# Mamba-style scan kernel: own prologue, own last image and a new instruction order

## The chip, the cores and the metric

The program runs on one core of one Trainium2 chip. The metric is the device time of that core in microseconds (us), the median of several runs. A core has five engines that run in parallel, each through its own list of instructions in strict order: PE (TensorE, matrix products), DVE (VectorE), ACT (ScalarE), POOL (GpSimd) and SP (SyncE, which here only issues DMAs). They wait for each other through semaphores. PE, DVE and ACT reach PSUM, POOL only SBUF.

## The reference, cut to what matters

There are 16 images of 16 x 16 positions (L = 256) with 64 channels. Each goes through a small self-attention with max-pooled keys and values, and a residual. Then it is read in four orders (as it is, columns reversed, rows reversed, both); every order is a sequence of 256 steps through a gated state-space mixer with 128 channels and 16 states per channel. All is fp32.

```
attn = softmax(theta @ maxpool(phi).T);  x = x + sigma * ((attn @ maxpool(g)) @ w_o + b_o)
hs, gate = split(rmsnorm(x) @ W_in.T);   hs = silu(causal_conv4(hs) + conv_b)
dt_r, B, C = split(hs @ W_x.T);          dt = softplus(dt_r @ W_dt.T + b_dt)
state = exp(dt * A) * state + dt * B * hs      # per time step, for 16 states n
y = sum_n(state * C) + hs * Dp
h = x + (y * silu(gate)) @ W_out.T;      out = layernorm(mean of 4 orders of rmsnorm(h))
```

## The kernel before, in words

The four orders of an image lie side by side as one row of T = 1024 elements, the 128 channels are the partitions. Per image and state n (16 states) the kernel needs a decay exp(a_n * dt), an input du * B_n (du = dt * hs), a scan over 1024 elements by DVE (`scan`, L1136 or L1143), a product with C_n, and an addition into `ps_y`, which PE does with identity matmuls (`sum_state`, L582). B_n and C_n come by DMA as 512 KB rows broadcast to 128 partitions (`load_b`, `load_c`).

`KIND = "ACCPACCCCPACPACC"` gives each state its kind:

- C: ACT writes the decay to PSUM (`ps_decay`, L804), POOL makes the input (`scan_input`, L1006), DVE scans in PSUM and DVE multiplies by C_n (`product`, L1150).
- P: the same inputs, but the scan writes to SBUF and POOL multiplies (L1012).
- A: ACT scales eight transposed blocks (`act_input`, L834), PE turns them into PSUM (`turn_input`, L568), the decay goes to SBUF (`sb_decay`, L811), DVE scans, POOL multiplies.

So an image has 16 scans, 9 DVE products, 7 POOL products, 12 POOL inputs and 4 inputs by ACT and PE. States of even and odd n alternate between the two buffers `ps_x[0]` and `ps_x[1]`, so state n can be prepared only when state n-2 has left its buffer.

The order of the work is written out by hand for every engine, in `prologue`, `steps(b, done, coming, later)` and `finish`. While image b is scanned, the image before it (`done`) is gated and normalised (`gated`, `hid_norm`, `out_norm` on DVE, `hid_squares`, `hid_inverse`, `out_squares`, `out_inverse`, `out_copy` on ACT, `hid_proj`, `hid_mean`, `out_mean` and others on PE), the next (`coming`) goes through norm, padding, convolution, gate and softplus, and the one after that (`later`) through its attention. All of these small stages share `ps_w`, whose halves are `w0` and `w1`. ACT changes its function table between Exp/Ln, Silu and Softplus (`silu_table`, `exp_table`, `softplus`).

In the prologue the first image goes through all stages with nothing to overlap. POOL makes its du (`scan_weight`), ACT copies all four parts of the padded input (`pad`), and the attention of the second image uses the first half of `ps_x[1]`. `warm(count)` issues matmuls of a zero tile into `ps_x[0]`, results unused; a matmul of fp32 is two instructions in the trace.

Of the kernel before, what the change touches and what calls it, by code (L numbers as in the profile page):

```python
# [5 lines left out]
ALU = mybir.AluOpType  # L6
# [4 lines left out]
L = SIDE * SIDE  # L11
# [3 lines left out]
N = 16  # L15
# [20 lines left out]
BY_POOL_IN = [n for n in range(N) if KIND[n] in "CP"]  # L36
BY_DVE_OUT = [n for n in range(N) if KIND[n] == "C"]
BY_ACT_IN = [n for n in range(N) if KIND[n] == "A"]
BY_SB_DECAY = [n for n in range(N) if KIND[n] == "A"]
BY_POOL_OUT = [n for n in range(N) if KIND[n] in "AP"]  # L40
NPI, NAI, NDO, NPO = len(BY_POOL_IN), len(BY_ACT_IN), len(BY_DVE_OUT), len(BY_POOL_OUT)
NSD = len(BY_SB_DECAY)
# [37 lines left out]
def build(nc, a, out):  # L80
    ctx = ExitStack()
    with ctx:
# [183 lines left out]
        def attn_bank(j):  # L266


            return ps_x[1][:, 0:HALF] if j.num == 1 else w0

        def product_wait(b, n):

            if n < 0:
                b, n = b + -1, n + N
            if KIND[n] == "C":
                return dve_products, NDO * b.num + BY_DVE_OUT.index(n) + 1
            return pool_products, NPO * b.num + BY_POOL_OUT.index(n) + 1

        def x_free_wait(b, n):

            if n < 0:
                b, n = b + -1, n + N
            if KIND[n] == "C":
                return dve_products, NDO * b.num + BY_DVE_OUT.index(n) + 1
            return scans, N * b.num + n + 1

        def pool_in_index(b, n):
            return NPI * b.num + BY_POOL_IN.index(n)

        def act_in_index(b, n):  # L290
            return NAI * b.num + BY_ACT_IN.index(n)

        def sb_decay_index(b, n):
            return NSD * b.num + BY_SB_DECAY.index(n)

        def scan_count(kind, each, index):

            return N * (index // each) + kind[index % each] + 1 if index >= 0 else 0

        def program(eng, prologue, steps, finish):  # L300

            prologue()
            for i in range(IMAGES):
                steps(Image(i), Image(i - 1) if i > 0 else None, Image(i + 1) if i + 1 < IMAGES else None,
                      Image(i + 2) if i + 2 < IMAGES else None)
            finish(last)
# [3 lines left out]
        def _(sp):  # L313
# [11 lines left out]
            def store_bc(j):  # L325

                all_at_least(sp, (bc_rows_done, j.num + 1), (pool_inputs, NPI * (j.num - 1)),
                             (pool_products, NPO * (j.num - 1)), (dve_products, NDO * (j.num - 1)))
# [4 lines left out]
            def load_b(b, n):  # L333

                i = pool_in_index(b, n)
# [15 lines left out]
            def prologue():  # L351
# [7 lines left out]
                load_c(first, 1)  # L359
                load_b(first, 5)  # L360

            def finish(j):
                store_out(j)

            def steps(b, done, coming, later):
                load_c(b, 2)
                load_b(b, 6)
                load_b(b, 7)
                load_c(b, 3)
                load_c(b, 4)  # L370
                load_b(b, 8)
                load_b(b, 9)
                load_c(b, 5)
                load_c(b, 6)
                if later:
                    load_x(later)
                load_b(b, 11)
                load_c(b, 7)
                load_b(b, 12)
                load_b(b, 14)  # L380
                load_c(b, 8)
                load_c(b, 9)
                load_b(b, 15)
                load_c(b, 10)
                if coming:
                    store_bc(coming)
                load_c(b, 11)
                load_c(b, 12)
                if coming:
                    load_b(coming, 1)  # L390
                    load_b(coming, 2)
                load_c(b, 13)
                load_c(b, 14)
                load_c(b, 15)
                if coming:
                    load_b(coming, 3)
                    load_c(coming, 0)
                    load_b(coming, 5)
                    load_c(coming, 1)
                if done:  # L400
                    store_out(done)

# [5 lines left out]
        def _(pe):  # L408
# [151 lines left out]
            def turn_input(b, n):  # L560

                i = act_in_index(b, n)
                pe.wait_ge(a_scaled, i + 1)
                if b.num == 0 and n % 2 == 1:
                    pe.wait_ge(x2_done, 2)
# [10 lines left out]
            def sum_state(b, n):  # L576

                at_least(pe, *product_wait(b, n))
                if n == 0:
                    at_least(pe, yg_done, 2 * b.num)  # L580
                for half in range(2):
# [5 lines left out]
            def prologue():  # L587
                second = first + 1
                pe.wait_ge(warm_zeroed, 1)
                warm(6)  # L590
                pe.wait_ge(qkv_weights_in, 16)
                qkv(first)
                pe.wait_ge(attn_weights_in, 16)
                scores(first)
                warm(2)
                warm(2)
                attn_turn(first)
                attn_out(first)
# [13 lines left out]
                warm(2)  # L612
                scores(second)
                bt_turn(first)
                warm(1)
                dut_turn(first, 0)
                dut_turn(first, 1)
                attn_turn(second)
                warm(1)
                attn_out(second)  # L620
                turn_input(first, 0)

            def finish(j):
                sum_state(j, 13)
# [5 lines left out]
                hid_mean(j)  # L630
                warm(2)
                warm(2)
                out_mean(j)
                warm(3)
                out_square(j)
# [657 lines left out]
```

## Time and profile before

| | |
|---|---|
| median of 3 runs | 848.98 us (848.57 to 849.10) |
| the profiled execution | 847.56 us |
| its span in the trace | 845.8 us |
| busy: PE, DVE, ACT, POOL | 93%, 93%, 90%, 89% |
| DVE idle until its first scan | 36.63 us |
| after the last product of DVE | 15.2 us |

The profiled execution lies 1.42 us below the median. The trace shows three stretches: a prologue until the first scan at 36.63 us, 15 image periods of about 49.7 us, then the last image (first scan at 782.02 us) and a tail of small steps that follow one another.

In the rows, a line gives the start in us, the duration in us, the engine, the line in the kernel, the operation, out<-in with the shape, and how many instructions were merged. Square brackets hold the idle time of that engine just before, and what ended it.

### The profile page before, as it was taken

What the parts mean: (1) busy time and instruction counts of PE and PEld (TensorE: products, weight loads), DVE (VectorE), ACT (ScalarE), POOL (GpSimd) and SP (SyncE); (2) the same over time, 40 slices, a digit from 0 to 9 for tenths busy, and PEclk for the clock granted to TensorE, in tenths of its full rate; (3) what the DMA queues carried; (4) which work ended last, traced back from release to release, by engine and by line L of the source; (5) the groups of instructions that cost most, each with busy time, mean ns of one, the idle gap of its engine ahead of it and who ended that gap; (6) DMA issues with size and microseconds to landing.
All of it is one profiled execution on the core that took longest, in us unless ns stands there. A gap on an engine that the chain in (4) does not pass through costs nothing.

```text
span 845.8 us, 10516 instructions
## 1 busy us (share of the span) xinstructions
PE 789.4 (93%) x2738; PEld 398.5 (47%) x2738; DVE 787.5 (93%) x537; ACT 759.9 (90%) x1438; POOL 748.6 (89%) x346
## 2 busy tenths in 40 slices
PE   7599999999999999999999999999999999999787
PEld 4335454454544445444454544444454554445343
DVE  2299999999999999999999999999999999999993
ACT  4899999999999999999999999999999999998551
POOL 0499999999989999998999999899999989999980
PEclk7899999999999999999999999999999999999999
DMA  1698999899998898989888898988989899888970
GB/s 46 248 292 295 294 314 300 300 292 307 315 286 308 301 294 284 321 300 310 307 293 293 294 312 305 293 305 309 305 280 312 282 312 312 297 295 293 302 265 6
DMA packets 73706, 240.61 MB, mean 284 GB/s; under 512 B 12848, under 2 KB 16176, under 8 KB 73648
## 3 DMA queue, kind: packets, MB, share of 16 engines
q1 hardware_dynamic: 73648, 239.96, 84.5%
q8 instruction: 22, 0.36, 0.2%
q14 instruction: 36, 0.29, 0.1%
HBM read 236.78 MB, written 3.15 MB: 284 GB/s over the span
## 4 chain that ended last, share of the span: by engine, by line
DMA 23%; ACT 23%; issue 16%; DVE 15%; POOL 13%; PE 8%; SPq 2%; ACTq 0%; DVEq 0%; POOLq 0%
DMA c_all<-bc_dram 13%; ACT scaled L834 10%; DMA b_all<-bc_dram 10%; POOL inp L1006 9%; ACT ps_x L804 6%; DVE state L1136 5%; DVE ps_x L1143 4%; PE ps_y L582 3%; POOL state L1012 3%; DVE state L1150 3%; DVE state L1143 2%; PE ps_w L473 1%; ACT ps_w L721 1%; SPq L343 1%; ACT oln L863 1%
## 5 line engine op out<-in xcount | busy, mean ns | idle before, releaser
L582 PE MATMUL ps_y<-state,packed 128*128 128x512 f32 x1024 | 473.2, 598 | 5.9 <-POOL state L1012 5.8
L1006 POOL TENSOR_TENSOR inp<-du,b_all 128x1024 f32<-128x1024 f32 x192 | 450.4, 2366 | 2.1 <-DMA b_all<-bc_dram 1.9
L1143 DVE TENSOR_TENSOR_SCAN ps_x<-ps_x,inp 128x1024 f32<-128x1024 f32 x144 | 325.6, 2281 | 3.4 <-ACT ps_x L804 3.4
L1012 POOL TENSOR_TENSOR state<-state,c_all 128x1024 f32<-128x1024 f32 x112 | 263.5, 2360 | 36.1 <-DVE state L1136 33.1
L582 PEld LDWEIGHTS ps_y<-state,packed 128*128 128x128 f32 x1024 | 191.4, 191 | 214.4 <-issue 196.9
L804 ACT ACTIVATE ps_x<-step,a_neg 128x1024 f32<-128x1024 f32 x192 | 213.8, 1114 | 43.4 <-DVE state L1150 21.9
L1150 DVE TENSOR_TENSOR state<-ps_x,c_all 128x1024 f32<-128x1024 f32 x144 | 172.2, 1214 | 1.8
L834 ACT ACTIVATE scaled<-dut,bt 128x128 f32<-128x128 f32 x512 | 154.4, 391 | 0.0
L1136 DVE TENSOR_TENSOR_SCAN state<-decay,ps_x 128x1024 f32<-128x1024 f32 x64 | 145.0, 2265 | 9.4 <-PE ps_x L568 9.4
L1143 DVE TENSOR_TENSOR_SCAN state<-ps_x,inp 128x1024 f32<-128x1024 f32 x48 | 109.7, 2285 | 7.5 <-issue 3.5
L568 PE MATMUL ps_x<-packed,scaled 128*128 128x128 f32 x512 | 68.3, 277 | 10.9 <-ACT scaled L834 9.2
L473 PE MATMUL ps_w<-xpad,w_conv 128*128 128x512 f32 x128 | 64.2, 626 | 11.2 <-ACT ocen L858 9.0
L568 PEld LDWEIGHTS ps_x<-packed,scaled 128*128 128x128 f32 x512 | 57.2, 143 | 36.8 <-ACT scaled L834 22.8
L811 ACT ACTIVATE decay<-step,a_neg 128x1024 f32<-128x1024 f32 x64 | 71.2, 1137 | 0.0
L996 POOL TENSOR_TENSOR du<-step,u 128x1024 f32<-128x1024 f32 x16 | 37.8, 2364 | 37.5 <-ACT step L789 37.5
L776 ACT ACT_TABLE_LOAD x46 | 59.0, 1283 | 0.8
L473 PEld LDWEIGHTS ps_w<-xpad,w_conv 128*128 128x128 f32 x128 | 23.9, 197 | 43.1 <-issue 37.1
L773 ACT ACT_TABLE_LOAD x31 | 39.8, 1283 | 0.5
L573 PE MATMUL ps_y<-u,diag_d 128*128 128x512 f32 x64 | 32.7, 593 | 0.0
L486 PE MATMUL ps_w<-u,w_step 128*128 128x512 f32 x64 | 30.3, 595 | 0.5 <-ACT u L769 0.5
L520 PE MATMUL ps_w<-hsq,mean_w 128*128 128x512 f32 x32 | 18.0, 645 | 11.0 <-ACT hsq L842 10.9
L769 ACT ACTIVATE u<-ps_w,packed 128x512 f32<-128x512 f32 x32 | 22.0, 687 | 4.5 <-PE ps_w L473 4.2
(123 smaller groups left out, 622.2 us busy)
## 6 DMA issues: line engine op xcount, KB each, us to landing
c_all<-bc_dram SPq DMA_DIRECT2D x256, 512.0 KB, 5.9
b_all<-bc_dram SPq DMA_DIRECT2D x192, 512.0 KB, 6.4
bc_dram<-bc_rows SPq DMA_DIRECT2D x64, 32.0 KB, 2.2
xa<-in_x_t SPq DMA_DIRECT2D x16, 64.0 KB, 8.1
out<-ofin SPq DMA_DIRECT2D x16, 64.0 KB, 3.8
packed<-in_packed SPq DMA_DIRECT2D x1, 635.0 KB, 4.1
packed<-in_packed SPq DMA_DIRECT2D x1, 129.0 KB, 2.5
w_qkv<-in_w_qkv SPq DMA_DIRECT2D x1, 64.0 KB, 2.0
```

Source lines behind the costliest of these rows:

```text
L473: last = mm(ps_w[:, HALF * half:HALF * (half + 1)], w_conv[:, 2 * half + tap2, :], moved, start=(tap2 == 0), stop=(tap2 == 1))
L568: last = nc.tensor.transpose(ps_x[n % 2][:, 128 * k:128 * (k + 1)], scaled[i % A_RING][:, k, :], ident)
L582: last = mm(ps_y[:, HALF * half:HALF * (half + 1)], ident, state[n % H_RING][:, HALF * half:HALF * (half + 1)], start=(n == 0), stop=(n == ...
L776: act.preload_act_table_set(EXP_LN)
L804: f(ps_x[n % 2][:, :], step[b.buf][:, :], ACT.Exp, scale=a_neg[:, n:n + 1]).then_inc(ps_decay_done, 1)
L811: f(decay[i % D_RING][:, :], step[b.buf][:, :], ACT.Exp, scale=a_neg[:, n:n + 1]).then_inc(sb_decay_done, 1)
L834: last = f(scaled[i % A_RING][:, k, :], dut[b.buf][:, k, :], ACT.Copy, scale=bt[b.buf][:, at, row:row + 1])
L1006: tt(inp[i % IN_RING][:, :], du[b.buf][:, :], b_all[i % B_RING][:, :], ALU.mult).then_inc(pool_inputs, 1)
L1012: tt(state[n % H_RING][:, :], state[n % H_RING][:, :], c_all[n % C_RING][:, :], ALU.mult).then_inc(pool_products, 1)
L1136: v.tensor_tensor_scan(held, decay[i % D_RING][:, :], x, 0.0, ALU.mult, ALU.add).then_inc(scans, 1)
L1143: v.tensor_tensor_scan(held if KIND[n] == "P" else x, x, inp[i % IN_RING][:, :], 0.0, ALU.mult, ALU.add).then_inc(scans, 1)
L1150: v.tensor_tensor(state[n % H_RING][:, :], ps_x[n % 2][:, :], c_all[n % C_RING][:, :], ALU.mult).then_inc(dve_products, 1)
```

## The change

1. **State kinds per image.** `KINDS` gives the first 15 images the old string and the last image `"ACPPAPCCPPAAPACA"`: 6 A, 6 P and 4 C instead of 4 A, 3 P and 9 C. `finish` now holds the whole last image, with an order of its own.
2. **First image.** DVE makes du and sets the stops (`first_weight`), and copies the second of the two padded orders (`first_pad`). DVE's weight preparations come before `rms(first)`. `state_decay` on ACT and `step_weights` on PE come earlier.
3. **Second attention** uses the second half of `ps_y`, which is free until the first `sum_state`; that one now waits for `x2_done` of the second image, and the waits for it in `ps_decay` and `turn_input` are gone.
4. **Zero matmuls** in the prologue: counts 8, 2, 3, 4, 7 where they were 6, 2+2, 1, 2, 1, 1. In the tail 2, 3, 2, 2 where they were 2, 2+2, 3.
5. **Order in `steps`**, for every image, on all five queues.

```diff
+LAST_KIND = "ACPPAPCCPPAAPACA"
+KINDS = [KIND] * (IMAGES - 1) + [LAST_KIND]
-            return ps_x[1][:, 0:HALF] if j.num == 1 else w0
+            return ps_y[:, HALF:T] if j.num == 1 else w0
@@ PE prologue
-                warm(6)
+                warm(8)
                 pe.wait_ge(qkv_weights_in, 16)
                 qkv(first)
+                warm(2)
                 pe.wait_ge(attn_weights_in, 16)
                 scores(first)
-                warm(2)
-                warm(2)
+                warm(3)
+                step_weights()
                 attn_turn(first)
                 attn_out(first)
+                warm(4)
                 pe.wait_ge(zeroed, 9)
                 mean_square(first)
-                step_weights()
-                warm(1)
-                qkv(second)
+                warm(7)
                 pe.wait_ge(conv_weights_ready, 1)
                 conv(first, 0)
                 conv(first, 1)
@@ DVE, new functions
+            def first_pad(j):
+                dve.wait_ge(zeroed, 9)
+                dve.wait_ge(xn_done, j.num + 1)
+                v.tensor_copy(grid(xpad[0:C, 1, 3:3 + L]), ordered(xn[j.buf][0:C, :], 1)).then_inc(padded, 1)
+                v.tensor_copy(grid(xpad[C:, 1, 2:2 + L]), ordered(xn[j.buf][C:, :], 1)).then_inc(padded, 1)
+            def first_weight(j):
+                dve.wait_ge(step_done, j.num + 1)
+                dve.wait_ge(u_done, 2 * (j.num + 1))
+                v.tensor_tensor(du[j.buf][:, :], step[j.buf][:, :], u[j.buf][:, :], ALU.mult).then_inc(du_done, 1)
```

The new order of one image in `steps`, with sN a scan, PN a DVE product, pN a POOL product, iN a POOL input, dN a `ps_decay`, a mark ' for the coming image:

```
DVE before: s0 s1 rms' gated P1 s2 P2 hid_norm s3 s4 s5 s6 P5 P6 s7 s8 P7 P8 s9 s10 s11 P11 pooling s12 s13 row_max s14 out_norm P14 s15 P15
DVE after:  P15(done) s0 s1 s2 gated P1 P2 rms' s3 s4 hid_norm s5 P5 s6 P6 s7 P7 s8 P8 s9 s10 s11 pooling P11 s12 s13 s14 row_max P14 s15 out_norm
ACT before: residual' d1 rms_inverse' d2 sb4 in10 hid_squares pad' hid_inverse d3 silu_table conv_silu0' exp_table d5 out_squares d6 silu_table conv_silu1' gate' exp_table d7 d8 softplus' exp_table bc_copy' d9 sb10 sb13 bt' dut0' d11 d12 theta dut1' in13 in0' d14 out_inverse softmax d15 attn_copy in4' out_copy sb0'
ACT after:  d2 residual' in10 rms_inverse' hid_squares d3 pad' hid_inverse d5 silu_table conv_silu0' exp_table out_squares d6 d7 silu_table conv_silu1' gate' exp_table d8 softplus' exp_table d9 bc_copy' sb10 sb13 d11 bt' dut0' in13 d12 theta dut1' in0' d14 sb0' sb4' out_inverse d15 softmax in4' d1' out_copy attn_copy
POOL before: p3 i8 p4 i9 i11 du' i12 i14 p9 p10 i15 p12 i1' p13 i2' p0' i3' i5' i6' i7'
POOL after:  p3 p4 i8 i9 i11 i12 du' i14 p9 p10 i15 p12 p13 i1' i2' i3' i5' p0' i6' i7'
```

On PE, `attn_out` comes at the head of the next image, `sum_state(13)` and `sum_state(14)` at the end of their own, `sum_state(b, 0)` before `hid_mean(done)`, and `scores(later)` before `turn_input(b, 13)`. On SP the loads are issued in an order that follows the others, some of the coming image's C rows earlier.

The last image, in `finish`:

```
DVE:  P15(done) s0 s1 P1 gated s2 s3 s4 s5 s6 s7 P6 P7 hid_norm s8 s9 s10 s11 out_norm s12 s13 s14 s15 P14
POOL: p2 p3 p4 p5 i8 i9 i12 p8 p9 i14 p10 p11 p12 p13 p15
PE:   ... sum12 sum13 sum14 sum15, then the tail as before
```

## Rows read from the trace of the kernel before

**Rows 1.** The page, busy time of each engine over the whole span.

```profile
PE 789.4 (93%) x2738; PEld 398.5 (47%) x2738; DVE 787.5 (93%) x537; ACT 759.9 (90%) x1438; POOL 748.6 (89%) x346
```

**Rows 2.** Stretches: length, busy PE, PEld, DVE, ACT, POOL, granted clock, DMA share, GB/s.

```profile
11.40:15.80 4.40, 3.41 (x8) 1.75 (x8) 2.27 (x10) 2.61 (x7) 0.00 (x0) 0.51 0.05 15
15.80:21.40 5.60, 5.56 (x7) 2.48 (x8) 1.01 (x5) 2.48 (x4) 0.00 (x0) 0.50 0.00 0
...
633.14:682.95 49.81, 47.93 (x169) 24.27 (x168) 48.82 (x33) 47.55 (x91) 46.70 (x22) 1.00 0.93 301
```

**Rows 3.** Timeline of DVE in a middle image, with its waits.

```profile
613.27 2.29 DVE L1143 TENSOR_TENSOR_SCAN state<-ps_x,inp 128x1024 f32<-128x1024 f32 x1 [0.17 <-issue]
...
633.14 2.29 DVE L1136 TENSOR_TENSOR_SCAN state<-decay,ps_x 128x1024 f32<-128x1024 f32 x1
...
638.11 1.29 DVE L1161 TENSOR_TENSOR yg<-ps_y,gate 128x512 f32<-128x512 f32 x2 [0.18 <-PE ps_y L582]
...
640.44 2.29 DVE L1143 TENSOR_TENSOR_SCAN ps_x<-ps_x,inp 128x1024 f32<-128x1024 f32 x1
642.76 1.23 DVE L1150 TENSOR_TENSOR state<-ps_x,c_all 128x1024 f32<-128x1024 f32 x1
...
644.84 2.29 DVE L1143 TENSOR_TENSOR_SCAN state<-ps_x,inp 128x1024 f32<-128x1024 f32 x1 [0.25 <-POOL inp L1006]
...
656.19 4.48 DVE L1143 TENSOR_TENSOR_SCAN ps_x<-ps_x,inp 128x1024 f32<-128x1024 f32 x2 [0.19 <-ACT ps_x L804]
...
663.09 2.29 DVE L1143 TENSOR_TENSOR_SCAN state<-ps_x,inp 128x1024 f32<-128x1024 f32 x1 [0.17 <-issue]
```

**Rows 4.** Timeline of ACT in the same image.

```profile
640.15 0.60 ACT L842 ACTIVATE hsq<-ps_w 128x512 f32<-128x512 f32 x1
...
654.97 2.25 ACT L804 ACTIVATE ps_x<-step,a_neg 128x1024 f32<-128x1024 f32 x2 [0.37 <-DVE state L1150]
...
659.66 1.28 ACT L776 ACT_TABLE_LOAD   x1
661.07 0.39 ACT L796 ACTIVATE bc_rows<-ps_w 128x256 f32<-128x256 f32 x1
661.88 1.12 ACT L804 ACTIVATE ps_x<-step,a_neg 128x1024 f32<-128x1024 f32 x1 [0.43 <-DVE state L1150]
```

**Rows 5.** Timeline of POOL in the last image: four inputs in a row.

```profile
786.68 9.32 POOL L1006 TENSOR_TENSOR inp<-du,b_all 128x1024 f32<-128x1024 f32 x4
```

**Rows 6.** Timeline of the prologue, PE and ACT.

```profile
1.05 2.93 PE L419 MATMUL ps_x<-warm_zero 128*128 128x128 f32 x12 [1.05 <-DVE warm_zero L1063]
...
3.77 1.05 PE L427 MATMUL ps_w<-xa,w_qkv 128*72 128x256 f32 x2
...
11.42 1.11 PE L458 MATMUL ps_w<-x2sq,mean_w 128*128 128x256 f32 x2 [1.10 <-ACT x L747]
...
15.28 0.41 ACT L762 ACTIVATE xpad<-xn 64x256 f32<-64x256 f32 x1
...
15.84 6.61 PE L473 MATMUL ps_w<-xpad,w_conv 128*128 128x512 f32 x8 [1.00 <-ACT xpad L762]
...
25.81 1.11 ACT L789 ACTIVATE step<-ps_w,packed 128x1024 f32<-128x1024 f32 x1 [0.80 <-PE ps_w L486]
```

**Rows 7.** Timeline of DVE: scan 9 of the first image, scan 0 of the second.

```profile
65.73 2.29 DVE L1143 TENSOR_TENSOR_SCAN state<-ps_x,inp 128x1024 f32<-128x1024 f32 x1 [0.16 <-issue]
...
85.37 2.28 DVE L1136 TENSOR_TENSOR_SCAN state<-decay,ps_x 128x1024 f32<-128x1024 f32 x1
```

**Rows 8.** Timeline of the last image, DVE and PE.

```profile
782.02 2.28 DVE L1136 TENSOR_TENSOR_SCAN state<-decay,ps_x 128x1024 f32<-128x1024 f32 x1
...
827.09 5.55 PE L582 MATMUL ps_y<-state,packed 128*128 128x512 f32 x12
...
829.38 1.22 DVE L1150 TENSOR_TENSOR state<-ps_x,c_all 128x1024 f32<-128x1024 f32 x1
...
832.68 1.29 DVE L1161 TENSOR_TENSOR yg<-ps_y,gate 128x512 f32<-128x512 f32 x2 [2.08 <-PE ps_y L582]
```

More of the change, by code:

```diff
@@ L35, with numbered, scans_until, before @@
 KIND = "ACCPACCCCPACPACC"
[L36 to L42, printed above, removed]
+LAST_KIND = "ACPPAPCCPPAAPACA"
+KINDS = [KIND] * (IMAGES - 1) + [LAST_KIND]
+def numbered(kinds):
+    return {key: i for i, key in enumerate((b, n) for b in range(IMAGES) for n in range(N) if KINDS[b][n] in kinds)}
+def scans_until(table, index):
+    return next(N * b + n + 1 for (b, n), i in table.items() if i == index) if index >= 0 else 0
+def before(table, num):
+    return sum(1 for b, n in table if b < num)
+POOL_IN, ACT_IN = numbered("CP"), numbered("A")
+DVE_OUT, POOL_OUT = numbered("C"), numbered("AP")
 EXP_LN, SILU, SOFTPLUS = "natural_log_exp_and_others", "silu_and_others", "softplus"
@@ L611, in prologue @@
                 step_proj(first, 0)
-                warm(2)
+                bt_turn(first)
+                qkv(second)
+                dut_turn(first, 0)
                 scores(second)
-                bt_turn(first)
-                warm(1)
-                dut_turn(first, 0)
                 dut_turn(first, 1)
+                turn_input(first, 0)
                 attn_turn(second)
-                warm(1)
-                attn_out(second)
-                turn_input(first, 0)
             def finish(j):
+                done = j + -1
+                sum_state(done, 15)
+                hid_residual(done)
+                hid_proj(done)
+                hid_mean(done)
+                turn_input(j, 4)
+                sum_state(j, 0)
+                sum_state(j, 1)
+                sum_state(j, 2)
+                sum_state(j, 3)
+                sum_state(j, 4)
+                sum_state(j, 5)
+                out_mean(done)
+                sum_state(j, 6)
+                out_square(done)
+                turn_input(j, 10)
+                skip(j, 0)
+                sum_state(j, 7)
+                turn_input(j, 11)
+                sum_state(j, 8)
+                sum_state(j, 9)
+                out_final(done)
+                turn_input(j, 13)
+                skip(j, 1)
+                sum_state(j, 10)
+                turn_input(j, 15)
+                sum_state(j, 11)
+                sum_state(j, 12)
                 sum_state(j, 13)
@@ L668, in steps @@
                 sum_state(b, 6)
+                turn_input(b, 10)
                 if coming:
                     bt_turn(coming)
-                turn_input(b, 10)
+                skip(b, 0)
                 if coming:
                     dut_turn(coming, 0)
-                skip(b, 0)
-                if later:
-                    qkv(later)
                 sum_state(b, 7)
@@ L679, in steps @@
                     dut_turn(coming, 1)
+                if later:
+                    qkv(later)
                 sum_state(b, 8)
-                sum_state(b, 9)
-                turn_input(b, 13)
                 if later:
                     scores(later)
+                turn_input(b, 13)
+                sum_state(b, 9)
                 if done:
@@ L697, in steps @@
                 if later:
-                    attn_out(later)
+                    attn_turn(later)
+                if done:
+                    out_final(done)
+                sum_state(b, 13)
+                sum_state(b, 14)
             program(pe, prologue, steps, finish)
@@ L933, in steps @@
                 ps_decay(b, 6)
+                ps_decay(b, 7)
                 if coming:
@@ L1195, in steps @@
             def steps(b, done, coming, later):
+                if done:
+                    product(done, 15)
                 scan(b, 0)
                 scan(b, 1)
-                if coming:
-                    rms(coming)
+                scan(b, 2)
                 if done:
```

309 lines of the change are left out of this document (193 added, 116 removed).

## The prediction, made before the changed kernel had run

> **What bounds the kernel now.** I read the page's busy times first [rows 1]: four engines lie between 89% and 93%, so none can be picked by its share alone. The stretches come next. In a middle image of 49.81 us DVE is busy 48.8 us, PE 47.9, ACT 47.6 and POOL 46.7 [rows 2]. DVE has about 1 us left, but it is not all there is: a timeline of DVE shows four short waits in the image, of 0.17 to 0.25 us, for PE, POOL and ACT [rows 3]. Each costs a little more than it shows, since the overlap with the next instruction is lost too (scan 3 starts 0.33 us later than its work asks), about 1.2 us together. DVE is the bound, with ACT right behind it: the reader should see that ACT runs 21.7 us from `hid_squares` to the decay of state 9 with waits of only 0.37 and 0.43 us [rows 4]. The last place is the prologue: no scan until 36.63 us, and in it a convolution of 6.61 us at half the granted clock [rows 2, 6].
>
> So the change has four accounts: prologue, first image, 14 middle images, last image. The sum goes by the profiled execution (span 845.8 us, time 847.56 us); the median of the runs is 1.42 us above it, and I add that at the end.
>
> **Prologue.** All steps from the first matmul to the end of softplus (26.92 us, [rows 6]) follow one another, so each counts in full.
> - 8 instead of 6 zero matmuls stand ahead of `qkv(first)`. Twelve instructions ran from 1.05 to the start of `qkv` at 3.77; they are 0.21 us apart, so four more cost 0.85 us. If the clock rises meanwhile, `qkv`'s two instructions (1.05 us) give up to 0.4 back. I take +0.7.
> - The zero matmuls and `step_weights` behind `qkv`, `scores` and `attn_out` fall in waits of PE for ACT and DVE; nothing late. The preparations of weights that DVE now does before `rms` take some 3 us and stand in DVE's idle time before it; the two earlier small steps of ACT likewise.
> - `mean_square` took 1.11 us at the half clock (0.51 in this stretch, [rows 2]); at full clock half of it: -0.5.
> - ACT makes two of four pads, DVE the others beside it. No row has a copy of 64x256 by DVE from SBUF; ACT's takes 0.41 [rows 6]. Between nearly nothing and the same as ACT it stays hidden: -0.9.
> - `conv(first)`: eight instructions at 0.85 us. The clock was at 0.50 from 11.5 us on, after a stretch in which PE had little to do, and it rose only at 21.5 us, after 5.7 us without a gap [rows 2]. With 4 and 7 zero matmuls around `mean_square` (8 and 14 instructions, 0.9 and 1.5 us at full clock, both shorter than the waits that they fill) PE has work in about two thirds of that time. In the tail of the last image, where zero matmuls stand in the same way, it kept the full clock. Then the convolution takes 8 x 0.43 = 3.4 us: -3.0.
> Sum -3.7 us. The other end: the clock falls all the same. Then seven zero matmuls take 14 x 0.21 = 3.0 us and delay the convolution by some 0.5 us, but PE works without a gap from 12.1 us on, the clock comes back in the middle of the convolution, and the net is -1.8; at worst +0.4.
>
> A rule of the Trainium skill bears on it, in "TensorE: Matmul & The Clock Gate", Part 1: the throttled clock is the default, activity of the array releases it, and the moment varies from run to run. By that rule zero operands do as well as real ones, and the prologue gives the 3.7 us; the same section makes the amount uncertain from run to run. The rows of the convolution agree with the first half.
>
> **First image.** From the end of softplus ACT has its work nearly without a gap until the decay of state 9: scan 9 started 38.8 us behind softplus, scan 0 of the second image another 19.64 us later [rows 7, 6]. DVE's du is 1.2 us faster than POOL's 2.3 (no row has it from two SBUF operands; the product of 1.22 us from PSUM is nearest, [rows 8]), and POOL gets one input more before its first product, but ACT is what is late next, and its list holds the same instructions. The copy of B and C rows now comes behind the decay of state 9 (0.4 us), and two product waits go later in the image (below, 0.24 us). I take -0.8, between 0 and -2.
>
> **Middle images.** DVE's own list is the same in content; removed waits could give 1.1 us per image. But the order adds waits of its own. I work the loop out from scan 0:
> - Scan 0 to `gated`: three scans at 2.19 us apart (the pair in [rows 3], less overlap) instead of two scans and `rms`: 6.57 us; before, it was 638.11 - 633.14 = 4.97.
> - `gated` to `hid_squares` on ACT, by PE's projection: 640.15 - 638.11 = 2.04 us.
> - From `hid_squares` to the decay of state 9 ACT has the very same instructions before and after (decays 3, 5, 6, 7, 8, pads, `hid_inverse`, both convolution Silus, gate, softplus, five table loads), only `bc_copy` has gone behind. Before: to the end of the last table load 659.66 + 1.28 - 640.15 = 20.79 us, less the wait of 0.37 = 20.42. The decay itself 1.10 and 0.12 to the start of the scan: 21.64 us.
> So scan 9 starts 6.57 + 2.04 + 21.64 = 30.25 us behind scan 0. By DVE's own work it could start at about 29.1 us: DVE now waits about 1.1 us for ACT, in two parts, before scan 6 (some 0.5, for decay 6, which stands behind the first Silu block) and before scan 9 (some 0.5). Before it was 663.09 - 633.14 = 29.95.
> - Scan 9 to the next scan 0: 633.14 - 613.27 = 19.87 us before. Products 11 and 15 no longer stand right behind their own scans; a product right behind costs 2.32 us from scan to product [rows 3] against 2.19: 19.87 - 0.24 = 19.63.
> The period is 30.25 + 19.63 = 49.88 us against 29.95 + 19.87 = 49.82. Over 14 images +0.8 us. PE's, POOL's and SP's parts have room in this timing: `hid_mean` is ready about 0.5 us before ACT asks, `turn_input(13)` 0.4 us before scan 13, loads of C are issued 7 us or more ahead. Range -0.3 to +0.3 us an image, that is 4 us each way.
>
> **Last image.** Five products go from DVE to POOL, two inputs from POOL to ACT and PE. DVE loses 5 x 1.13 us. POOL gains: behind scan 13 of image 14 it has p13, five operations of transition (four inputs, p0), and 16 more until p13 of the last: 22 at 2.32 us [rows 5] = 51.0 us without a gap. Scan 13 ends 5.7 us before P15 of image 14, so p13 of the last image ends 45.4 us behind the start of that P15. Then PE adds three states, 12 instructions in 5.2 us [rows 8]: 50.6. Before, the same stretch ran from 780.9 (1.14 before scan 0) to 832.4, 0.3 before `gated`: 51.5 [rows 8]. Gain -0.9 us: POOL takes DVE's place as the bound. If POOL were earlier, DVE would set it, with its stalls for decays and for `turn_input(11)` (1.6 us by the same walk): scan 15 ends at 44.2, its product by POOL 2.4, a sum 1.7: 48.3, so -3.2. The other end is 0. The tail behind keeps its steps; the zero matmuls there stand in waits: 0.
>
> **Sum.** -3.7 - 0.8 + 0.8 - 0.9 = -4.6 us. 847.56 - 4.6 = 843.0 for a profiled execution, 844.4 against the median.
>
> **Rivals.**
> 1. *The clock is not kept in the prologue.* For it: between `mean_square`'s zero matmuls and the pads PE still has about 1 us idle, and it fell there before. The prologue gives 1.8 or nothing: 846.3 to 848.5.
> 2. *ACT does not bind the middle images*, DVE runs without waits at about 48.8 us: another 14 x 1.0 us, 830. Against it speaks that ACT's 47.6 us plus its waits for scan 0 (0.6) and for the projection (1.2) already fill the period.
> 3. *`sum_state(b, 0)` before `hid_mean` makes it slower.* PE now waits for POOL's product 0 before it may run `hid_mean`, and product 0 stands behind four inputs of POOL instead of two. By my walk it ends 8.0 us behind P15, PE asks at 9.7 us, and ACT can bear another 0.6 us. From 10.3 us on, one POOL operation (2.3 us) late, every further tenth goes through `hid_inverse` into the ACT chain above and so into every image. With 0.5 us beyond it: +7 us, 851.4. Against it: POOL has about 2.7 us idle per image with which to catch up.
> 4. *The last image is set by DVE after all*: 842.1.
>
> **Chances.** Forecast 0.53, its own range 840 to 848 (14 images by 0.3 us make nearly all of it); rival 1 0.17; rival 2 0.08; rival 3 0.14; rival 4 0.08. The range reaches from half-way to rival 2 to rival 3: 836.5 to 851.5. A measurement of this kernel can tell 0.2%, 1.7 us, from no change. Faster than 847.3: most of the forecast (0.48), rivals 2 and 4, half of rival 1: 0.72. Slower than 850.7: rival 3, of which a part stays below, and a tail of the forecast: 0.13. Within: 0.15.
>
> **What would show it.** In the prologue: granted clock 1.00 through the convolution and softplus ending near 23.2 us. In a middle image: waits of DVE for `ps_x` of ACT before scans 6 and 9, none of note before 3 and 7; `hid_squares` 8.6 us behind scan 0; a period of 49.6 to 50.2. In the last image: POOL without a gap until its last product, DVE waiting little, first scan to last `gated` near 49.7 us instead of 50.7. The prediction is wrong if the waits before scans 6 and 9 are missing or a third appears, for PE or POOL.

## The result: slower by a quarter of a per cent

| | before | changed |
|---|---|---|
| median of 13 runs each | 849.07 us | 850.71 us |
| ratio of the times | | 1.0024, 95% interval 1.0015 to 1.0033 |
| the profiled execution, its span | 847.56, 845.8 us | 849.61, 847.7 us |
| first scan | 36.63 us | 33.22 us |
| scan 0 of the second image | 85.37 us | 80.92 us |
| from there to scan 0 of the last image, 14 images | 696.65 us | 703.97 us |
| from there to the last `gated` | 50.66 us | 49.69 us |
| tail behind it | 13.1 us | 13.1 us |

The prediction was 844.4 us and faster; the kernel became slower, by 1.6 us in the medians and by 2.0 us in the ratio and in the profiled executions. Each ratio here and below is to runs of the kernel before that were taken together with the experiment (medians of 847.85 to 849.26 us), and it need not be the quotient of the two medians.

The four accounts of the prediction say where. The start gained 4.45 us, the last image 0.97, the tail nothing, and the 14 middle images lost 7.3: together +1.9 us, the difference of the two spans. Of the 7.3 us, 14 times the longer period (50.30 instead of 49.82 us) is 6.7; one of the 14 images took 50.57 us, and what that one waited for was not followed up.

The page of the changed kernel has nearly the same busy times as [rows 1]; DVE has less to do and a longer span around it:

```profile
PE 791.7 (93%) x2772; PEld 403.6 (48%) x2772; DVE 783.2 (92%) x536; ACT 765.7 (90%) x1452; POOL 754.0 (89%) x347
```

The same stretches as in [rows 2]: the first convolution, a middle image, the last image up to its `gated` (columns as there).

```profile
15.38:19.05 3.67, 3.67 (x9) 1.74 (x10) 0.00 (x0) 1.84 (x2) 0.00 (x0) 1.00 0.00 0
...
583.93:634.23 50.30, 48.15 (x169) 24.41 (x168) 48.85 (x34) 47.72 (x92) 46.77 (x22) 1.00 0.85 298
...
784.89:834.58 49.69, 45.66 (x143) 21.15 (x142) 42.17 (x26) 28.17 (x55) 46.48 (x21) 1.00 0.62 217
```

DVE is busy 48.85 us in a middle image, as before; the image is 50.30 us long instead of 49.82. Which waits make up the rest is in DVE's timeline, the counterpart of [rows 3]:

```profile
583.93 2.27 DVE L1236 TENSOR_TENSOR_SCAN state<-decay,ps_x 128x1024 f32<-128x1024 f32 x1
...
590.48 1.26 DVE L1261 TENSOR_TENSOR yg<-ps_y,gate 128x512 f32<-128x512 f32 x2
...
603.55 2.30 DVE L1243 TENSOR_TENSOR_SCAN ps_x<-ps_x,inp 128x1024 f32<-128x1024 f32 x1 [0.73 <-ACT ps_x L853]
...
614.41 2.29 DVE L1243 TENSOR_TENSOR_SCAN state<-ps_x,inp 128x1024 f32<-128x1024 f32 x1 [0.38 <-ACT ps_x L853]
...
630.57 2.30 DVE L1243 TENSOR_TENSOR_SCAN ps_x<-ps_x,inp 128x1024 f32<-128x1024 f32 x1 [0.20 <-ACT ps_x L853]
...
634.23 2.27 DVE L1236 TENSOR_TENSOR_SCAN state<-decay,ps_x 128x1024 f32<-128x1024 f32 x1
```

The waits before scans 6 and 9 (603.55 and 614.41) are the two that were forecast. A third, before scan 15, was not. All three are for a decay by ACT, whose timeline answers to [rows 4]:

```profile
592.49 0.60 ACT L891 ACTIVATE hsq<-ps_w 128x512 f32<-128x512 f32 x1 [0.94 <-PE ps_w L537]
...
613.21 1.12 ACT L853 ACTIVATE ps_x<-step,a_neg 128x1024 f32<-128x1024 f32 x1
...
629.37 1.10 ACT L853 ACTIVATE ps_x<-step,a_neg 128x1024 f32<-128x1024 f32 x1
...
644.67 0.42 ACT L812 ACTIVATE xpad<-xn 64x256 f32<-64x256 f32 x1 [0.26 <-DVE xn L1213]
```

The last of these lines is of the next image; in this one ACT waits the same 0.26 us for `xn`, until 594.36. So the loop is: scan 0 to `gated` 6.55 us, to `hid_squares` 2.01, to scan 9 21.92, to the next scan 0 19.82; sum 50.30. The prediction had 6.57, 2.04, 21.64 and 19.63.

The prologue, PE, DVE and ACT, the counterpart of [rows 6]:

```profile
1.05 3.78 PE L444 MATMUL ps_x<-warm_zero 128*128 128x128 f32 x16 [1.05 <-DVE warm_zero L1149]
...
4.63 1.06 PE L452 MATMUL ps_w<-xa,w_qkv 128*72 128x256 f32 x2
...
12.29 0.67 PE L483 MATMUL ps_w<-x2sq,mean_w 128*128 128x256 f32 x2 [0.21 <-ACT x L798]
12.79 1.72 PE L444 MATMUL ps_x<-warm_zero 128*128 128x128 f32 x14
...
14.45 0.29 DVE L1218 COPY xpad<-xn 64x256 f32<-64x256 f32 x1
...
15.38 3.67 PE L498 MATMUL ps_w<-xpad,w_conv 128*128 128x512 f32 x8 [0.86 <-ACT xpad L813]
...
22.42 1.11 ACT L840 ACTIVATE step<-ps_w,packed 128x1024 f32<-128x1024 f32 x1 [0.80 <-PE ps_w L511]
...
23.57 1.23 DVE L1224 TENSOR_TENSOR du<-step,u 128x1024 f32<-128x1024 f32 x1 [2.61 <-ACT step L840]
```

Every step is there: 0.86 us later at `qkv`, `mean_square` in 0.67 us instead of 1.11, the convolution in 3.67 instead of 6.61, DVE's copies of 0.29 us beside ACT's pads, softplus at its end at 23.53 us instead of 26.92.

DVE's scan 9 of the first image and scan 0 of the second (as [rows 7]):

```profile
61.58 2.29 DVE L1243 TENSOR_TENSOR_SCAN state<-ps_x,inp 128x1024 f32<-128x1024 f32 x1
...
80.92 2.28 DVE L1236 TENSOR_TENSOR_SCAN state<-decay,ps_x 128x1024 f32<-128x1024 f32 x1
```

And the last image (as [rows 8]), with POOL's last products:

```profile
784.89 2.27 DVE L1236 TENSOR_TENSOR_SCAN state<-decay,ps_x 128x1024 f32<-128x1024 f32 x1
...
834.58 1.29 DVE L1261 TENSOR_TENSOR yg<-ps_y,gate 128x512 f32<-128x512 f32 x2 [5.66 <-PE ps_y L606]
...
819.77 11.60 POOL L1086 TENSOR_TENSOR state<-state,c_all 128x1024 f32<-128x1024 f32 x5
```

### The profile page after: what moved, and what is told of

The parts are those of the page before. It is cut to its first block, busy times and chain, and to the rows that moved or that the text cites. A ratio compares the mean times of both kernels' runs of the same rounds, so it can differ in the third digit from the quotient of the medians.

```text
span 847.7 us, 10597 instructions
## 1 busy us (share of the span) xinstructions
PE 791.7 (93%) x2772; PEld 403.6 (48%) x2772; DVE 783.2 (92%) x536; ACT 765.7 (90%) x1452; POOL 754.0 (89%) x347
## 4 chain that ended last, share of the span: by engine, by line
PE 28%; ACT 20%; DMA 16%; DVE 13%; issue 11%; POOL 10%; SPq 2%; DVEq 0%; ACTq 0%; POOLq 0%
PE ps_y L606 13%; DMA b_all<-bc_dram 10%; POOL inp L1080 7%; DMA c_all<-bc_dram 6%; DVE ps_x L1243 6%; ACT ps_x L853 5%; PE ps_w L498 4%; POOL state L1086 3%; DVE state L1250 3%; PE ps_w L537 2%; ACT scaled L883 2%; PE ps_w L511 2%; ACT L827 2%; ACT xpad L813 1%; DVE state L1243 1%
## 5 line engine op out<-in xcount | busy, mean ns | idle before, releaser
L1080 POOL TENSOR_TENSOR inp<-du,b_all 128x1024 f32<-128x1024 f32 x190 | 445.2, 2362 | 44.3 <-DMA b_all<-bc_dram 26.5
L1243 DVE TENSOR_TENSOR_SCAN ps_x<-ps_x,inp 128x1024 f32<-128x1024 f32 x139 | 315.8, 2281 | 13.8 <-ACT ps_x L853 13.8
L1086 POOL TENSOR_TENSOR state<-state,c_all 128x1024 f32<-128x1024 f32 x117 | 273.6, 2358 | 29.5 <-DVE state L1243 28.6
L1250 DVE TENSOR_TENSOR state<-ps_x,c_all 128x1024 f32<-128x1024 f32 x139 | 167.6, 1214 | 2.2
L883 ACT ACTIVATE scaled<-dut,bt 128x128 f32<-128x128 f32 x528 | 161.0, 392 | 0.5
L1236 DVE TENSOR_TENSOR_SCAN state<-decay,ps_x 128x1024 f32<-128x1024 f32 x66 | 149.7, 2268 | 7.7 <-PE ps_x L591 7.7
L1243 DVE TENSOR_TENSOR_SCAN state<-ps_x,inp 128x1024 f32<-128x1024 f32 x51 | 116.2, 2279 | 5.8 <-ACT ps_x L853 5.3
L591 PEld LDWEIGHTS ps_x<-packed,scaled 128*128 128x128 f32 x528 | 61.9, 142 | 32.1 <-issue 27.8
L891 ACT ACTIVATE hsq<-ps_w 128x512 f32<-128x512 f32 x16 | 9.6, 597 | 29.0 <-PE ps_w L537 29.0
L537 PE MATMUL ps_w<-yg,packed 128*64 128x256 f32 x128 | 20.0, 405 | 9.9 <-DVE yg L1261 9.9
```

The costliest lines, as they stand in the source:

```text
L591: last = nc.tensor.transpose(ps_x[n % 2][:, 128 * k:128 * (k + 1)], scaled[i % A_RING][:, k, :], ident)
L883: last = f(scaled[i % A_RING][:, k, :], dut[b.buf][:, k, :], ACT.Copy, scale=bt[b.buf][:, at, row:row + 1])
L1080: tt(inp[i % IN_RING][:, :], du[b.buf][:, :], b_all[i % B_RING][:, :], ALU.mult).then_inc(pool_inputs, 1)
L1086: tt(state[n % H_RING][:, :], state[n % H_RING][:, :], c_all[n % C_RING][:, :], ALU.mult).then_inc(pool_products, 1)
L1236: v.tensor_tensor_scan(held, decay[i % D_RING][:, :], x, 0.0, ALU.mult, ALU.add).then_inc(scans, 1)
L1243: v.tensor_tensor_scan(held if KINDS[b.num][n] == "P" else x, x, inp[i % IN_RING][:, :], 0.0, ALU.mult, ALU.add).then_inc(scans, 1)
```

## The experiments on the middle images

Two theories stood against each other. **Chain**: one loop, from scan 0 over `gated`, PE's projection, ACT's list to decay 9, then DVE's list to the next scan 0, sets the period; a change counts by what it does to this loop. **Local**: each wait of DVE costs what it shows, and what DVE doesn't wait for costs nothing.

### xn one product earlier

```diff
                 product(b, 1)
-                product(b, 2)
                 if coming:
                     rms(coming)
+                product(b, 2)
```

> The changed kernel with one step moved on DVE in the middle images: the norm of the coming image (xn) stands between products 1 and 2 instead of behind product 2. In the trace of the changed kernel ACT waits 0.26 us for xn ahead of its pads, while DVE itself loses nothing there. Theory A (chain): what counts is the chain scan 0, gated, hid_squares, ACT's list, decay 9, scan 9; the 0.26 us stand on it, so the image period falls from 50.30 to about 50.04 us, scan 9 comes 0.26 us earlier behind scan 0, and the time falls by 14 x 0.26 = 3.6 us. Theory B (only DVE's own waits count): the waits of DVE are before scans 6, 9 and 15, none near xn; the order of two DVE steps changes nothing, period 50.3, time as the changed kernel.

Measured: 845.50 us, ratio to before 0.9967 (0.9957 to 0.9978). Scans 0, 9 and 0 on DVE:

```profile
581.84 2.27 DVE L1236 TENSOR_TENSOR_SCAN state<-decay,ps_x 128x1024 f32<-128x1024 f32 x1
...
611.97 2.29 DVE L1243 TENSOR_TENSOR_SCAN state<-ps_x,inp 128x1024 f32<-128x1024 f32 x1 [0.38 <-ACT ps_x L853]
...
631.79 2.27 DVE L1236 TENSOR_TENSOR_SCAN state<-decay,ps_x 128x1024 f32<-128x1024 f32 x1
```

The period is 49.95 us instead of 50.30, all of it between scan 0 and scan 9 (30.13 instead of 30.48), although DVE had no wait at the place that was changed. The wait of ACT for xn stood on the chain. It gave 0.35 us, 0.09 more than the wait itself shows. The same step on ACT, without the wait:

```profile
590.90 1.11 ACT L853 ACTIVATE ps_x<-step,a_neg 128x1024 f32<-128x1024 f32 x1
591.95 0.40 ACT L812 ACTIVATE xpad<-xn 64x256 f32<-64x256 f32 x1
```

From the start of this decay to the start of the first pad ACT takes 1.05 us, where the changed kernel took 1.37 (592.99 to 594.36): the wait of 0.26 and 0.06 of lost overlap. The four pads behind it take 1.74 us instead of 1.77. Local falls.

### Decay 6 earlier, so that DVE's largest wait goes

```diff
                 ps_decay(b, 5)
+                ps_decay(b, 6)
                 if coming:
                     silu_table(coming)
                     conv_silu(coming, 0)
                     exp_table(coming)
                 if done:
                     out_squares(done)
-                ps_decay(b, 6)
                 ps_decay(b, 7)
```

> The changed kernel with decay 6 on ACT moved ahead of the first Silu block, so that it is there long before scan 6. Theory A (chain): ACT has as much to do ahead of decay 9 as before, and now waits about 0.3 us for scan 4 before decay 6. The wait of DVE before scan 6 (0.73 us) goes, but DVE waits that much longer before scan 9; scan 9 starts at the same distance behind scan 0 or 0.3 us later (30.5 to 30.8 us); the period is 50.3 to 50.6 us, the time 0 to 4 us above the changed kernel. Theory B (each wait has its own cost): the period falls by 0.8 us to 49.5, the time by 11 us.

Measured: 860.56 us, ratio 1.0145 (1.0121 to 1.0169), the slowest of all. On DVE the wait of 0.73 us is gone; scans 0, 8, 9 and 0:

```profile
592.88 2.27 DVE L1236 TENSOR_TENSOR_SCAN state<-decay,ps_x 128x1024 f32<-128x1024 f32 x1
...
618.98 2.30 DVE L1243 TENSOR_TENSOR_SCAN ps_x<-ps_x,inp 128x1024 f32<-128x1024 f32 x1 [0.28 <-ACT ps_x L853]
...
623.95 2.29 DVE L1243 TENSOR_TENSOR_SCAN state<-ps_x,inp 128x1024 f32<-128x1024 f32 x1 [1.41 <-ACT ps_x L853]
...
643.76 2.27 DVE L1236 TENSOR_TENSOR_SCAN state<-decay,ps_x 128x1024 f32<-128x1024 f32 x1
```

It has come back before scans 8 and 9, as 0.28 and 1.41 us. Scan 9 starts 31.07 us behind scan 0 instead of 30.48, and the period is 50.88. ACT now waits itself before decay 6:

```profile
607.82 1.12 ACT L853 ACTIVATE ps_x<-step,a_neg 128x1024 f32<-128x1024 f32 x1 [0.38 <-DVE state L1236]
```

0.38 us of the 0.59 are this wait; 0.06 a decay that is followed by a table load instead of another decay (1.12 instead of 1.06 us on ACT), and 0.12 a wait of softplus for PE that opened. The chain had forecast a period of 50.3 to 50.6 us and was a little low; on the time it was well low, with 0 to 4 us above the changed kernel against 9.9 measured. The 14 periods are 8.1 us of that, and the first image, which goes through the same order, lost 1.6 more. Local, with a period of 49.5 and a time 11 us lower, had the wrong sign.

### Decay 15 earlier

```diff
-                if done:
-                    out_inverse(done)
                 ps_decay(b, 15)
+                if done:
+                    out_inverse(done)
```

> The changed kernel with decay 15 on ACT moved ahead of out_inverse. DVE waits 0.20 us before scan 15 for it. Theory A: behind scan 9 DVE is the chain, so this wait costs in full, with the lost overlap 0.28 us an image: period 50.02, time lower by 3.9 us. Rival: the wait only moves, ACT's list until decay 1 of the next image stays as long, and scan 1 or 2 of the next image waits instead: period 50.3.

Measured: 846.25 us, ratio 0.9981 (0.9969 to 0.9992); period 50.01 us instead of 50.30 (scan 0 at 582.57 and 632.58), the wait before scan 15 gone, those before 6 and 9 unchanged at 0.73 and 0.38. Scans 0, 15 and 0 on DVE:

```profile
582.57 2.27 DVE L1236 TENSOR_TENSOR_SCAN state<-decay,ps_x 128x1024 f32<-128x1024 f32 x1
...
628.93 2.28 DVE L1243 TENSOR_TENSOR_SCAN ps_x<-ps_x,inp 128x1024 f32<-128x1024 f32 x1
...
632.58 2.27 DVE L1236 TENSOR_TENSOR_SCAN state<-decay,ps_x 128x1024 f32<-128x1024 f32 x1
```

Behind scan 9 DVE itself is the chain, and its wait counts in full. This is one case in which the local reading happens to be right.

### gated earlier

```diff
-                scan(b, 2)
+                product(b, 1)
                 if done:
                     gated(done)
-                product(b, 1)
-                product(b, 2)
+                scan(b, 2)
                 if coming:
                     rms(coming)
+                product(b, 2)
```

> The changed kernel with DVE's order at the head of an image scan 0, scan 1, product 1, gated, scan 2, xn, product 2 (it was scans 0, 1, 2, gated, products 1, 2, xn). gated now starts 5.6 us behind scan 0 instead of 6.55. Theory A: hid_squares comes about 0.9 us earlier; of that ACT gives some back by waits for xn (0.2), scan 3 (0.3) and product 5, so scan 9 starts about 30.1 us behind scan 0 instead of 30.48; period 49.9, time lower by some 5 us. If the order at the head were without effect on the chain (rival: ACT's own list bounds the period, wherever it starts), the period would stay at 50.3.

Measured: 845.57 us, ratio 0.9963 (0.9949 to 0.9978), period 49.93. DVE, scan 0, `gated`, scan 9:

```profile
581.75 2.27 DVE L1236 TENSOR_TENSOR_SCAN state<-decay,ps_x 128x1024 f32<-128x1024 f32 x1
...
587.38 1.28 DVE L1261 TENSOR_TENSOR yg<-ps_y,gate 128x512 f32<-128x512 f32 x2
...
611.86 2.29 DVE L1243 TENSOR_TENSOR_SCAN state<-ps_x,inp 128x1024 f32<-128x1024 f32 x1 [0.61 <-ACT ps_x L853]
```

`gated` came 0.92 us earlier behind scan 0, scan 9 only 0.37: ACT waited for xn (0.15) and for scan 3 (0.27), as the expectation said. The third wait that it named, for product 5, shows only in the length of decays 6 and 7, 2.37 us together instead of 2.14.

## The experiments on the prologue

### The new prologue alone, in the kernel before

Edit: points 2 to 4 of the change up to the first scan, with middle and last image as before. Not all of the changed prologue is in it: ACT still makes decay 1 behind both `act_input`, and POOL and SP keep their old orders.

> The kernel before, with the new prologue alone (zero matmuls, weight preparations early, half of the pads and du by DVE, second attention in ps_y); middle and last image as before. Theory A: the prologue's gain is real and independent of the rest. Softplus of the first image ends 1.8 to 3.4 us earlier than 26.92 (depending on whether the clock falls between 10 and 16 us in that execution, as it did in four of the five traces of changed kernels so far), the image period stays 49.82, and the time is 2 to 3.5 us below before. Rival: the first image is bound by loads or by ACT's list from its start, so the second image begins no earlier than 85.4 us and the time is that of before within 0.5 us.

Measured: 849.37 us, ratio 1.0015 (1.0004 to 1.0026): slower, so the expectation of theory A failed, and the rival's place was wrong too. The first scan is at 33.09 us, 3.5 us earlier than before, and the period is 49.82. But the second image is later than before (`gated` at 90.91 instead of 90.07 us). In between, on DVE and ACT:

```profile
38.06 2.30 DVE L1151 TENSOR_TENSOR_SCAN ps_x<-ps_x,inp 128x1024 f32<-128x1024 f32 x1 [2.69 <-ACT ps_x L799]
...
50.59 2.29 DVE L1144 TENSOR_TENSOR_SCAN state<-decay,ps_x 128x1024 f32<-128x1024 f32 x1 [1.81 <-PE ps_x L566]
...
49.13 0.69 ACT L766 ACTIVATE u<-ps_w,packed 128x512 f32<-128x512 f32 x1 [1.43 <-PE ps_w L473]
```

Scan 1 waits for a decay that ACT's old order has behind two `act_input`: of the 3.5 us, 1.2 are left at scan 1 (38.06 instead of 39.29 us). Then scan 4 and the Silu wait for PE, which runs at the half clock just then: 0.50 from 46 to 50 us, where the kernel before had 1.00. The four instructions of its convolution take 3.78 us instead of 1.99, and scan 4 starts at 50.59 instead of 49.73 us.

```profile
46.00:50.00 4.00, 4.00 (x10) 2.02 (x9) 2.29 (x1) 2.54 (x4) 2.18 (x2) 0.50 0.86 273
```

In the changed kernel decay 1 stands ahead of the first `act_input`, and scan 1 follows scan 0 at once (35.42 us). So 2.3 us of the gain went to the place of decay 1, and 1.9 to the half clock in the first image. The first is a matter of order. That the clock falls there in every execution is not shown, since one was profiled; the median of 12 runs lies above before all the same. Two later images also took 50.10 us instead of 49.82, for a reason that was not looked for.

### The old zero matmuls in the changed kernel

```diff
-                warm(8)
+                warm(6)
                 pe.wait_ge(qkv_weights_in, 16)
                 qkv(first)
-                warm(2)
                 pe.wait_ge(attn_weights_in, 16)
                 scores(first)
-                warm(3)
+                warm(4)
                 step_weights()
                 attn_turn(first)
                 attn_out(first)
-                warm(4)
                 pe.wait_ge(zeroed, 9)
                 mean_square(first)
-                warm(7)
+                warm(1)
```

> The changed kernel with the zero matmuls of the old counts at their places (6 ahead of qkv, none behind, 4 behind scores, none behind attn_out, 1 ahead of the convolution). Theory A: granted clock 0.50 in the convolution of the first image, which takes 6 us or more instead of 3.67; softplus ends 2 to 3.5 us later than in the changed kernel's median run, less the 0.85 us that the two zero matmuls ahead of qkv cost; time 1.5 to 3 us above the changed kernel. Rival: the clock recovers by itself, time as the changed kernel or 0.8 us below it.

Measured: 852.39 us, ratio to before 1.0044 (1.003 to 1.0058), 1.7 us above the changed kernel's median, as theory A had it. PE in the attention's output product (`gw`), in `mean_square` and in the convolution:

```profile
10.65 1.22 PE L475 MATMUL ps_w<-xa,gw 128*128 128x256 f32 x2 [0.47 <-ACT xa L788]
...
12.97 1.19 PE L483 MATMUL ps_w<-x2sq,mean_w 128*128 128x256 f32 x2 [1.10 <-ACT x L796]
...
16.57 5.22 PE L498 MATMUL ps_w<-xpad,w_conv 128*128 128x512 f32 x8 [1.99 <-ACT xpad L811]
```

All ran at half speed (the changed kernel has 0.70, 0.67 and 3.67 us), the convolution for half its length; theory A had expected 6 us or more for it. But this execution doesn't repeat what happened in the kernel before. There PE was fast from about 5.5 us and fell at 11.5; here it never became fast before the convolution (already the eight zero matmul instructions behind `scores` took 1.91 us instead of 1.06). So the time shows that the old counts cost 1.7 us. By which of the five places they do it, and whether they fail to raise the clock or to keep it, is not shown.

How safely they do it is another matter. The prologue up to decay 0 is the same in eight of the executions that were profiled; in three of these (the changed kernel, its new prologue alone, and the last version below) the granted clock stayed at 1.00 until 25 us or later, in the other five it fell at about 10 us and came back between 13.4 and 16.4, as in these two slices of the first experiment on the middle images:

```profile
10.00:11.00 1.00, 0.53 (x3) 0.34 (x2) 0.47 (x4) 0.38 (x1) 0.00 (x0) 0.57 0.00 0
12.00:13.00 1.00, 1.00 (x7) 1.00 (x7) 0.00 (x0) 0.84 (x2) 0.00 (x0) 0.50 0.00 0
```

The convolution took 3.67 us in all of them. But where the clock had fallen, the zero matmuls themselves were slow and stood in the way, and softplus ended at 24.6 to 25.1 us instead of 23.4 to 23.5. Five of eight is a rough share: four of the five are the experiments on the middle images, which ran together on one chip; of the other four, one fell, and the execution with du on POOL (below), whose PE list is the same, kept the clock until 26 us. The 13 runs of the changed kernel point the same way: six have a mean granted clock of 0.990 or more over their span and spans of 847.0 to 847.7 us, seven have 0.987 to 0.989 and spans of 848.7 to 851.0. The profiled execution of the changed kernel was one of the lucky ones; its time lies 1.1 us under the median. The Trainium skill ("TensorE: Matmul & The Clock Gate", Part 1) says that activity releases the throttle and that the moment varies from run to run; these traces show both.

### Pads and du, one at a time

```diff
-                pad(first, (0,))
+                pad(first)
```
```diff
-                first_weight(first)
```

The first also takes `first_pad` from DVE, the second gives `scan_weight(first)` back to POOL.

> The changed kernel with all four pads of the first image on ACT again. Theory: from the start of the first pad on ACT to the start of the convolution 1.9 us instead of 1.0, so softplus ends 0.9 us later than an execution of the changed kernel with the same clock. Rival: the table load, which ACT does behind its pads, was what the first Silu waited for, or PE was still at its zero matmuls; then less than 0.3 us.

> The changed kernel with du and the stops of the first image on POOL again. Theory: DVE's du takes 1.23 us, POOL's 2.34; scan 0 starts behind the chain du, stops, decay 0, act_input, turn_input, so from the end of softplus to scan 0 it takes about 10.3 us instead of 9.7, less than the full 1.1 us since ACT waits there only for part of it; to the second image's scan 0 57.4 us becomes about 58. Rival: ACT's list behind softplus hides all of it, no difference.

Measured in one execution each. Pads: from `mean_square` to softplus 11.01 us instead of 10.13, so 0.88 us later, and the second image as much. du: softplus at the same 22.42 us, the first scan at 34.36 instead of 33.22. ACT waits twice:

```profile
26.32 1.15 ACT L860 ACTIVATE decay<-step,a_neg 128x1024 f32<-128x1024 f32 x1 [0.70 <-POOL step L1072]
...
29.22 0.60 ACT L872 ACTIVATE dut<-ps_w 128x512 f32<-128x512 f32 x1 [0.26 <-PE ps_w L582]
```

Decay 0 stands ahead of the rest of ACT's list and now waits for POOL; it starts 0.79 us later. The other 0.35 us come from PE, whose transposes of du reach ACT's second copy late. In this execution the granted clock fell to 0.50 at 26.7 us, in the changed kernel's only behind 28 us, so how much of the 0.35 is the clock's is open. The second image is 1.14 us later as well: twice what was expected.

## The last image, and a version that beats both

```diff
-LAST_KIND = "ACPPAPCCPPAAPACA"
+LAST_KIND = "ACPPAPCCPPAACACA"
```

with product 12 of the last image on DVE behind scan 12, and gone from POOL's list.

> The changed kernel with the product of state 12 of the last image given back from POOL to DVE (kind C instead of P). Theory A (POOL bounds the last image): in the changed kernel POOL runs its last five products without a gap to 831.4 us, and PE cannot start the last three sums before 829.1. With one product less the last three sums start 2.3 us earlier, then scan 15 sets the last product; the stretch from scan 0 of the last image to its gated falls from 49.7 to about 48.5 us, time lower by 1.2 us. Rival (DVE bounds it): one product more on DVE, 1.1 us longer.

Measured: 850.29 us, ratio 1.002 (1.001 to 1.0029); the stretch between the last two `gated` is 43.92 us instead of 44.06. The gain is 0.14 us, not 1.2. POOL now waits 2.0 us before its last product, so it is no longer the bound, but nothing is won:

```profile
825.80 1.06 PE L591 MATMUL ps_x<-packed,scaled 128*128 128x128 f32 x8 [0.59 <-DVE state L1235]
826.70 8.75 PE L606 MATMUL ps_y<-state,packed 128*128 128x512 f32 x20
```

PE adds five states in one piece at the end. In its list `turn_input(15)` stands ahead of the sums of states 11 and 12; it waits for scan 13, which the new product made 1.1 us later, and the sums pile up behind it. POOL was the bound in the changed kernel, with PE's order right behind. That PE's order is what took the gain is read from this trace; no run moved `turn_input(15)`.

The combination of three edits (`gated` earlier, decay 15 earlier, state 12):

> The changed kernel with three changes together: the head of an image on DVE as scan 0, scan 1, product 1, gated, scan 2, xn, product 2; decay 15 ahead of out_inverse; state 12 of the last image with its product on DVE. Theory A (the chain by ACT's list to decay 9, then DVE's own list): the period is 49.93 - 0.28 = 49.65 us, below the 49.82 of before; with prologue (-2 to -3.4), 14 x -0.17 = -2.4, last image -2.2 against before, the time is 7 to 8 us below before. If the gains of the two orders were the same gain twice, the period would stay at 49.9 and the time about 4 us below before.

Measured: 842.49 us against 847.85 us of before, ratio 0.9928 (0.9915 to 0.9942). `gated` in two images that follow one another:

```profile
584.09 1.29 DVE L1260 TENSOR_TENSOR yg<-ps_y,gate 128x512 f32<-128x512 f32 x2
...
633.79 1.29 DVE L1260 TENSOR_TENSOR yg<-ps_y,gate 128x512 f32<-128x512 f32 x2
```

The period is 49.70 us, 0.05 above the forecast; the two gains add but for 0.06 us. The whole is 5.4 us faster than before in the medians and 6.1 by the ratio, less than the 7 to 8 expected. The two spans (839.9 and 845.8 us) say where: the start gave 3.9 us, the last image 1.1 instead of 2.2, and the 14 middle images 0.85 instead of 2.4, since the last three of them took 49.86, 49.82 and 49.47 us.

## Why the prediction was wrong, point by point

- **Prologue**, -3.7 us forecast: -3.4 in the profiled execution, and -1.8 to -2.3 in the five of eight in which the clock fell. Each of its terms was seen. What was underrated is the bounce of the clock: it was a rival with 0.17, and came in five of eight. Its price was 1.1 to 1.6 us, less than the 1.9 that the rival gave it at least.
- **First image**, -0.8: measured -1.06 (80.92 - 23.53 = 57.39 us instead of 85.37 - 26.92 = 58.45). The sum was near, but partly by luck. The note on du was wrong: it called ACT's list what is late next, and so gave DVE's faster du next to nothing; taking it away cost 1.14 us, more than the whole gain. So the other edits up to scan 9 gave nothing, where the copy of the B and C rows alone was to give 0.4. Scan 9 to the second image gave 0.30 us, 0.24 forecast.
- **Middle images**, +0.8: measured +7.3. This is the term that failed. The loop and its mechanism were right, both waits of DVE stood where they were forecast, and the first two legs are exact to 0.03 us. But the loop was summed as if no leg held any wait besides. Two were left out, both for a neighbour that was a little late: ACT waits 0.26 us for xn ahead of its pads, because `rms` on DVE now stands behind both products (moving it gave 0.35), and scan 15 waits 0.20 us for a decay that now stands behind two others and `out_inverse` (moving it gave 0.29). Together the two are 0.64 us, against 0.42 by which the period was missed; the other 0.22 us are the four legs, which the forecast had 0.02 to 0.10 us too long each. Without its wait the third leg is 21.56 us (21.64 forecast), the fourth 19.53 (19.63). An error of 0.42 us in a loop of 50 is small, but 14 times it is 5.9 of the 6.5 us that this account missed. The forecast allowed 0.3 us an image each way, and the sign hung on it. Its own sign of being wrong was a third wait of DVE, for PE or POOL; the third came, but for ACT.
- **Last image**, -0.9: measured -0.97, with POOL working its last five products without a gap. Bound and size were right. DVE was to wait little; it waited 5.66 us for PE's last sums, which is what a bound on POOL leaves to it.
- **Rival 3** (`sum_state(b, 0)` ahead of `hid_mean`) gave a time near the measured one by another mechanism. It did not happen: ACT takes `hln` at once behind its pads, with no wait for PE. The stated range reached up to 851.5 us for this rival's sake, so it is luck that 850.71 lies inside it.

## What to carry to other kernels

When an order is changed that repeats many times, walk the whole loop with every wait, on the helper engines too: here a wait of 0.26 us on ACT, which feeds DVE, cost 0.35 us an image, and one of 0.20 us on DVE itself 0.29. The size of a wait on the busiest engine doesn't say what can be won: taking away the one of 0.73 us made the image 0.58 us longer. Ask which loop it closes, and shorten a leg of that. And a gain at the start is kept only if the next stretch can be reached with it: with the first scan 3.4 us earlier the second image began 4.45 us earlier in the changed kernel, and with the first scan 3.5 us earlier it began 0.84 us later in the kernel with most of the new prologue and the old order behind it.

## What the runs showed of the hardware that was not expected

- The granted clock in the prologue differs between executions of the same instructions: all at 1.00 until 25 us or later, or 0.50 from about 10 us until 13.4 to 16.4 us, with softplus 1.1 to 1.6 us later.
- The column of the granted clock can be wrong. With the old zero matmuls it shows 1.00 from the start to beyond 20 us, while `mean_square` takes 1.19 us and the first convolution matmuls twice their time at full clock, as in the kernel before, where the column says 0.50. In the changed kernel too it shows 1.00 over the first 4 us, in which the zero matmul instructions start 0.22 us apart, against 0.12 us behind 12.8 us. Durations of matmuls of known size are the safer reading.
- DVE's product of two SBUF operands of 128x1024 took 1.23 us, as its product from PSUM (1.20 to 1.23); a copy of 64x256 from SBUF took 0.29 us, against 0.41 on ACT.
